# Post-norm decoder layer on one core: cross attention, routing and shared expert written as one stage

## The reference, cut to what matters

```python
x = _layernorm(x + _L0_attn_ref(x, Wq, bq, Wk, bk, Wv, bv, Wo, bo))      # 16 heads of 128, 4 KV heads
x = _layernorm(x + _L0_xattn_ref(x, ctx, ctx, Wh, wg_w, wo_w, gn_gamma, gn_beta))
x = _layernorm(x + _L0_ffn_ref(x, gate_weight, inv_mapping, ...))

def _L0_xattn_ref(x, k, v, Wh, wg_w, wo_w, gn_gamma, gn_beta):             # 2 heads of 128
    Q, K, V = (einsum('bshd,hde->bshe', t, Wh) for t in (xh, kh, vh))
    scores = einsum('bshe,bthe->bhst', Q, K) / sqrt(hd)
    A = maximum(abs((scores * Dn).sum(axis=0)), 1.0)        # summed over all 16 sequences
    O = einsum('hst,bthe->bshe', A, V)
    Y = (O - mu) / sqrt(var + GN_EPS) * gn_gamma + gn_beta
    return relu(x @ wg_w) * Y @ wo_w

def _moe_forward(x, ...):                                   # 64 routes, top 6, 8 experts of 8
    scores = softmax(x @ gate_weight.T)
    w_dense = the 6 largest of 64, the others 0
    flat = w_dense[:, inv_mapping]                          # (tokens, 8 experts, 8)
    scalar = flat.sum(-1)
    soft = softmax(where(flat == 0, -1e9, flat), axis=-1)   # the second softmax
    y = sum over f of scalar[f] * expert_f(x, soft[f])
    return y + silu(x @ sh_gate_W.T) * (x @ sh_up_W.T) @ sh_down_W.T      # + the shared expert
```

## Time and profile before

| what | us |
|---|---|
| three timed runs | 960.9, 962.25, 964.76; median 962.25 |
| the profiled execution | 962.09, of which the traced span is 960.2 |
| TensorE busy | 893.3 (93%) |
| VectorE, ScalarE, GpSimd busy | 654.8, 518.3, 370.9 |
| identity products of `keep_busy` in the cross stage (L57) | 120 instructions, 14.2 |

### The profile page before, as it was taken

One profiled execution on the slowest core, in us unless ns is written; L12 is line 12 of the kernel. 1 busy time (PEld: TensorE's weight loads), 2 busy tenths in 40 slices (PEclk: granted clock), 3 DMA queues, 4 the chain that ended last, 5 costly groups with the idle time before them and its releaser, 6 DMA issues. The chain is left out here.

```text
span 960.2 us, 16062 instructions
## 1 busy us (share of the span) xinstructions
PE 893.3 (93%) x5722; PEld 797.7 (83%) x5722; DVE 654.8 (68%) x1347; ACT 518.3 (54%) x1225; POOL 370.9 (39%) x261
## 2 busy tenths in 40 slices
PE   6899999999999999899789888999999999999992
PEld 5799999999999998777678786888888888888882
DVE  4656564656565565657758865778887888787885
ACT  4655555647464555214444326566656566666553
POOL 1721212213131312025424225474747465657430
PEclk9999999999999999999999999999999999999996
DMA  6300000000000000400010020202202020200002
GB/s 222 110 2 23 1 22 0 22 0 22 7 15 11 0 12 1 135 1 1 1 65 6 8 98 31 85 29 79 79 29 86 31 87 22 85 23 23 23 1 88
DMA packets 16430, 38.00 MB, mean 40 GB/s; under 512 B 2048, under 2 KB 6912, under 8 KB 15232
## 3 DMA queue, kind: packets, MB, share of 16 engines
q1 hardware_dynamic: 15744, 35.29, 10.8%
q0 software_dynamic: 640, 2.10, 0.7%
HBM read 34.76 MB, written 2.62 MB: 39 GB/s over the span
## 5 line engine op out<-in xcount | busy, mean ns | idle before, releaser
L241 POOL TENSOR_TENSOR att_probs<-att_probs,att_share 128x512 f32<-128x512 f32 x64 | 66.3, 1039 | 191.6 <-DVE att_share L525 191.6
L1491 POOL TENSOR_TENSOR all_xT_lo<-moe_inner,all_xT_lo 128x512 fp32r<-128x512 f32 x64 | 82.7, 1292 | 89.5 <-ACT all_xT_lo L1668 86.2
L429 ACT ACTIVATE att_probs<-att_score,att_bias 128x128 f32<-128x128 f32 x256 | 90.5, 380 | 41.9 <-DVE att_bias L516 41.7
L1483 POOL TENSOR_TENSOR all_xT_hi<-moe_xe,all_xT_hi 128x1024 fp32r<-128x1024 f32 x31 | 74.5, 2403 | 65.4 <-ACT all_xT_hi L1627 65.4
L1668 ACT ACTIVATE all_xT_lo<-moe_inner 128x512 fp32r<-128x512 f32 x64 | 40.4, 631 | 89.2 <-DVE moe_inner L1738 89.2
L562 DVE SCALAR_TENSOR_TENSOR att_OT_lo<-att_mix,att_bv,att_OT_hi 128x512 fp32r<-128x512 f32 x64 | 45.8, 750 | 58.1 <-ACT att_OT_hi L467 58.1
L467 ACT ACTIVATE att_OT_hi<-att_mix,att_bv 128x512 fp32r<-128x512 f32 x64 | 43.5, 703 | 65.9 <-PE att_mix L50 65.7
L48 PE MATMUL att_proj<-att_xT_hi,att_Wq_hi 128*128 128x256 f32 x256 | 74.8, 292 | 1.4 <-DVE att_Wq_lo L490 0.8
L48 PE MATMUL att_acc<-att_Wo_hi,att_OT_hi 128*128 128x256 f32 x256 | 73.0, 285 | 1.6 <-DVE att_OT_lo L562 1.6
L302 PEld LDWEIGHTS att_score<-att_KT,att_QT 128*128 128x128 f32 x512 | 62.5, 196 | 11.8 <-issue 8.6
L50 PE MATMUL att_proj<-att_xT_hi,att_Wq_lo 128*128 128x256 f32 x256 | 72.1, 281 | 0.0
(11 more groups left out here) (299 smaller groups left out, 2904.7 us busy)
## 6 DMA issues: line engine op xcount, KB each, us to landing
all_stage<-in_expert_w SPq DMA_DIRECT2D x8, 1152.0 KB, 5.1
moe_spread<-soft_dram SPq DMA_DIRECT2D x64, 128.0 KB
all_scale<-in_expert_scale SPq DMA_DIRECT2D x8, 320.0 KB, 5.4
att_xT<-in_xT SPq DMA_DIRECT2D x8, 256.0 KB, 3.1
att_stage<-in_Wq SPq DMA_DIRECT2D x4, 512.0 KB, 7.4
att_stage<-in_Wo SPq DMA_DIRECT2D x4, 512.0 KB, 5.4
att_x_tok<-in_x_tok POOLq DMA_DIRECT2D x8, 256.0 KB, 3.1
out<-all_r SPq DMA_DIRECT2D x4, 512.0 KB, 4.4
```

What stands on the lines that cost most here:

```text
L241: pool.tensor_tensor(p3, p3, each, ALU.mult).then_inc(prob_ready, 1)
L429: ins = act.activation(p_[:, c], score[b][:, c], ACT.Exp, bias=bias[b][:, h:h + 1], scale=SCALE, accum_out=m_[:, h:h + 1])
L1483: pool.tensor_tensor(xe[u % 2].lo[:, :], xe32[:, :], xe[u % 2].hi[:, :].bitcast(F32), ALU.subtract).then_inc(xe_lo, 1)
L1491: pool.tensor_tensor(innerT[u % 2].lo[at], inner[at], innerT[u % 2].hi[at].bitcast(F32), ALU.subtract).then_inc(inner_lo, 1)
```

## The change

The cross and route functions become one, `cross_and_route`, with one order per engine and no barrier between them.

- SyncE issues in this one stage: the context, `decay`, `gamma` and `beta` (now 2 values per partition each), `route_w` without the router's columns, the router's columns `Wr`, then `inv` and `rows`. VectorE's program for the stage begins with the wait for the last two, their two instructions and four memsets. Among them are `ln_eps` and `gn_eps`, which ScalarE waits for (`eps_ready`) before its first square root.
- The gates come out transposed (features on partitions). The normalised mix is turned instead of the gated product, and gamma and beta are applied by ScalarE on the way out of PSUM, with a scale and a bias per partition; before, GpSimd did that with two passes over broadcast copies.
- The square roots take the epsilon as a bias, so VectorE's additions of it go.
- The group norm's factors come in groups of 2, 2, 4, 4 and 4 tiles, and the last layer norm in groups of 2.
- All of `keep_busy` in the merged stage goes; those of the attention's end and of the experts' start stay.
- The second softmax is written once; ScalarE copies the turned result three times (high part twice, and the fp32 copy for DRAM) where it copied once, and VectorE drops a copy.
- The shared expert's next slices are put between the steps of routing, and `kept` is copied out by ScalarE.
- The first expert's weights are split in eight parts on GpSimd, one behind each low half.
- In the first turn of the attention the projections of Q2 stand before the second set of scores.
- In the experts `move_low` stands behind the unit's first SiLU.

```diff
@@ -336,6 +336,10 @@
 
                 for j in range(KV):
 
+                    if j == 0 and weights:
+                        pe.wait_ge(w_lo, j + 5)
+                        for what in step_units(j, last):
+                            projects(what)
                     if not (last and j == KV - 1):
 
                         for q_unit in ((-3, -2), (1, 2), (3, 4), (7, 8))[j]:
@@ -356,11 +360,9 @@
                             mm = pe.transpose(mix[b][:, h * S:(h + 1) * S], probs[j % 2][b][:, h * S:(h + 1) * S],
                                               ident[:, :])
                         mm.then_inc(pt_ready, 1)
-                    if j == 0 and weights:
-                        pe.wait_ge(w_lo, j + 5)
                     if j == 2 and not last:
                         pe.wait_ge(xT_lo, g + 2)
-                    if j != 1:
+                    if j > 1 or j == 0 and not weights:
                         for what in step_units(j, last):
                             projects(what)
...
         @block.sync
         def _(sp):
             for c in range(1, CHUNKS):
-                sp.dma_start(ctxT[c][:, :].rearrange("p (h t) -> p h t", h=XH),
+                sp.dma_start(ctxT[c].rearrange("p (h t) -> p h t", h=XH),
                              a["ctxT"][:, :, c * CT:(c + 1) * CT]).then_inc(ctx_in[c], 16)
-            sp.dma_start(decay[:, :], a["decay"]).then_inc(const_in, 16)
+            sp.dma_start(decay, a["decay"]).then_inc(const_in, 16)
             for dst, src in ((gamma, a["gamma"]), (beta, a["beta"])):
-                sp.dma_start(dst[:, :], src.rearrange("(o d) -> o d", o=1).to_broadcast([P, D])).then_inc(const_in, 16)
-            sp.dma_start(w32[:, :], a["route_w"]).then_inc(route_in, 16)
+                sp.dma_start(dst[:, :], src.rearrange("(k p) -> p k", k=DK), allow_slow_non_contiguous=True
+                             ).then_inc(const_in, 16)
+            sp.dma_start(w32[:, :], a["route_w"][:, DK * E:]).then_inc(route_in, 16)
+            sp.dma_start(Wr[:, :], a["route_w"][:, 0:DK * E]).then_inc(wr_in, 16)
+            sp.dma_start(inv_raw[:, :], a["inv"].rearrange("(o e) -> o e", o=1).to_broadcast([E, FK])).then_inc(small_in, 16)
+            sp.dma_start(rows[:, :], a["rows"]).then_inc(small_in, 16)
+            sp.wait_ge(route_lo, 1)
+            load_weights(sp, a, 0, stage, scale, expert_in)
+            by_parity = soft_dram.rearrange("(f two k) t -> two f k t", two=GROUPS, k=F)
+            for c in range(CHUNKS):
+                for n in range(GROUPS):
+                    sp.wait_ge(softT32_ready, GROUPS * c + n + 1)
+                    sp.dma_start(by_parity[n, :, :, c * CT:(c + 1) * CT], softT32[:, n * CT:(n + 1) * CT]).then_inc(stored, 16)
+                if c == CHUNKS - 2:
+                    sp.wait_ge(expert_ready, 1)
+                    load_weights(sp, a, 1, stage, scale, expert_in)
+            sp.wait_ge(stored, 16 * GROUPS * CHUNKS)
+            sp.wait_ge(expert_in, 64)
 
         @block.gpsimd
...
-            keep_busy(pe, bank[7], ident, 14)
 
...
-            gates(0, (0,))
-            pe.wait_ge(at_ready, 1)
-            mix_values(0)
-            gates(0, (1,))
-            mix_values(1)
-            keep_busy(pe, bank[4], ident, 8)
-            mix_values(2)
-            keep_busy(pe, bank[4], ident, 14)
...
+            pe.wait_ge(at_ready, 1)
+            mix_values(0)
+            mix_values(1)
+            gates(0)
+            for c in range(CHUNKS):
+                turn_mix(c)
+                if c < CHUNKS - 2:
+                    mix_values(c + 2)
+                if c:
+                    turn_x2(c - 1)
+                outputs(c)
+                if c < CHUNKS - 1:
+                    gates(c + 1)
...
+            shared_in(0, 0)
+            shared_in(0, 1)
+            logits(0)
             for i in range(2):
                 pe.wait_ge(turned2_lo, 2 * (CHUNKS - 2) + i + 1)
-            keep_busy(pe, bank[0], ident, 14)
             turn_x2(CHUNKS - 1)
-            keep_busy(pe, bank[0], ident, 10)
+            shared_in(0, 2)
+            for c in range(CHUNKS):
+                if c < CHUNKS - 1:
+                    shared_in(c + 1, 0)
+                turn_kept(c)
+                if c < CHUNKS - 1:
+                    shared_in(c + 1, 1)
+                flat(c)
+                if c == CHUNKS - 2:
+                    logits(c + 1)
+                shared_out(c)
+                if c < CHUNKS - 2:
+                    logits(c + 1)
+                if c < CHUNKS - 1:
+                    shared_in(c + 1, 2)
+                soft_out(c)
...
-            act.activation(gram[:, :], bank[4][:, 0:HH], ACT.Copy).then_inc(gram_out, 1)
-            act.wait_ge(var_ready, 1)
-            act.activation(std[:, :], var[:, :], ACT.Sqrt).then_inc(std_ready, 1)
+            act.activation(gram, bank[4][:, 0:HH], ACT.Copy).then_inc(gram_out, 1)
+            act.wait_ge(eps_ready, 2)
+            act.wait_ge(mv_ready, 1)
+            act.activation(std[:, :], mv2[:, :, 1], ACT.Sqrt, bias=ln_eps[:, 0:1]).then_inc(std_ready, 1)
             for n in range(0, 4 * CHUNKS, 2):
                 act.wait_ge(kv_ready, n + 1)
                 act.activation(kv_to(n), bank[n % 4][:, :], ACT.Copy).then_inc(kg_out, 1)
...
+            def affine(c):
+
+                if c == 0:
+                    act.wait_ge(const_in, 48)
+                for i in range(2):
+                    act.wait_ge(y_turned, 2 * c + i + 1)
+                    if c:
+                        act.wait_ge(wyt_out, 2 * (c - 1) + i + 1)
+                    for k in range(DK):
+                        at = slice(k * 2 * P, (k + 1) * 2 * P)
+                        ins = act.activation(YT[i][:, at], bank[4 + i][:, at], ACT.Identity, bias=beta[:, k:k + 1],
+                                             scale=gamma[:, k:k + 1])
+                    ins.then_inc(yt_out, 1)
...
+            def soft_high(c):
+                for n in range(GROUPS):
+                    act.wait_ge(soft_turned, GROUPS * c + n + 1)
+                    for at in (0, 2 * GR):
+                        ins = act.activation(softT[n][at:at + GR, c * CT:(c + 1) * CT], soft_bank[n][0:GR, :], ACT.Copy)
+                    if c:
+                        act.wait_ge(stored, 16 * GROUPS * c)
+                    act.activation(softT32[:, n * CT:(n + 1) * CT], soft_bank[n][0:GR, :], ACT.Copy
+                                   ).then_inc(softT32_ready, 1)
+
+            for n in (CHUNKS - 1, CHUNKS):
+                deviation(n)
+                normalise_x2(n)
+            shared(0, 0)
+            shared(0, 1)
+            exp1(0)
+            for i in range(2):
+                high_x2(2 * (CHUNKS - 1) + i)
+            shared(0, 2)
+            for c in range(CHUNKS):
+                if c < CHUNKS - 1:
+                    shared(c + 1, 0)
+                take_kept(c)
+                if c < CHUNKS - 1:
+                    shared(c + 1, 1)
+                exp2(c)
+                if c < CHUNKS - 1:
+                    exp1(c + 1)
+                    shared(c + 1, 2)
+                soft_high(c)
...
-                dve.wait_ge(mv_ready, n)
-                at = slice(tiles[0], tiles[-1] + 1)
-                dve.tensor_scalar(var[:, at], mv2[:, at, 1], LN_EPS, None, ALU.add).then_inc(var_ready, 1)
-
-            variance(range(B), 1)
+
+            dve.wait_ge(small_in, 32)
+            dve.tensor_copy(inv[:, :], inv_raw[:, :]).then_inc(inv_ready, 1)
+            dve.wait_ge(inv_ready, 1)
+            dve.tensor_scalar(onehot[:, :], inv[:, :], rows[:, 0:1], None, ALU.is_equal).then_inc(onehot_ready, 1)
+            dve.memset(s3[:, :, E:E + 1], 3.0).then_inc(sentinels, 1)
+            dve.memset(s3[:, :, E + 1:E + 2], 2.0).then_inc(sentinels, 1)
+            dve.memset(ln_eps[:, :], LN_EPS).then_inc(eps_ready, 1)
+            dve.memset(gn_eps[:, :], GN_EPS).then_inc(eps_ready, 1)
+            moments(range(B), 0)
             dve.wait_ge(std_ready, 1)
             dve.reciprocal(rstd[:, :], std[:, :]).then_inc(rstd_ready, 1)
             dve.wait_ge(rstd_ready, 1)
...
-                for copy in range(3):
-                    to = soft2[:, :].rearrange("p (t n c) -> p n t c", t=TT * GROUPS, n=3)[:, copy]
-                    ins = dve.tensor_tensor(to.rearrange("p t (f k) -> p t f k", k=F), four(e2[:, :]),
-                                            four(part2[:, :]).to_broadcast([P, TT * GROUPS, F // GROUPS, F]), ALU.mult)
-                ins.then_inc(soft2_ready, 1)
-            shared_out(CHUNKS - 2)
-            for n in range(GROUPS):
-                split_soft(CHUNKS - 1, n)
-            shared_out(CHUNKS - 1)
+                dve.tensor_tensor(soft2[:, :].rearrange("p (t k) -> p t k", k=F), e2_8, wide(part2, TT * F, F), ALU.mult
+                                  ).then_inc(soft2_ready, 1)
+
+            factors_x2(CHUNKS - 1)
+            variance(CHUNKS)
+            factors_x2(CHUNKS)
```

(27 more changed lines are left out.)

913 lines of the change are left out of this document (448 added, 465 removed).

## The result

The changed kernel takes 985.45 us (median of 4 runs, 984.1 to 986.77), the kernel before 961.88 in the same job. The ratio is 1.0229 (95% interval 1.0203 to 1.0255), so it is 2.3% slower. The prediction was 976.6 us with a range of 962 to 985. The direction and the main cause were right; the size was 8.9 us short. The time is 0.45 us past the upper end of the range; the ratio, laid on the 962.25 us from which the forecast started, gives 984.3 us, just inside.

What follows compares the result with a forecast made beforehand. No engine is full in the stages that merge; chains passing from engine to engine bound them. 962.09 + 0.6 + 12.9 - 6.5 + 1.8 + 2.0 + 3.7 = 976.6 us, range 962 to 985, likeliest case 970 to 982.

Steps and rivals of the forecast that it cites:

- The start of the stage: Merged stage's head: VectorE waits for late `inv` and `rows`, then for GpSimd's hold on the shared port; +12.9 us.
- else +1.3: Merged stage's head: extra if ScalarE's table load of 1.28 us before the root came in line, not beside.
- The bound of +15: Upper bound for the stage's start: every small load waits as `decay` did and the table load is in line.
- From `AT` to the last output: From `at_ready` to the last output product: fillers and GpSimd's passes gone, 49.0 us against 55.65; -6.5 us.
- From there to the experts: Last output product to the experts: barrier and fillers gone, longer chunk periods, earlier first chunk; +1.8 us.
- the three periods: Routing chunks, `flat` to `flat`: 19.5 us each against 18.0, since ScalarE and VectorE get more work; +4.5 us.
- Port and clock: Routing chunks: VectorE meets GpSimd on the port oftener and TensorE's clock falls without filler; +2.0 us.
- The third rival: Routing chunks: three more clock drops of 1.7 us and 3 us more of port, 984.7 us; chance 0.15.
- The experts: Experts stage: `move_low` behind the SiLU lengthens TensorE's wait for moved rows in seven units; +3.7 us.
- The attention's +0.6: Attention: Q2's projections ahead of the second scores make those scores late, partly given back later; +0.6 us.
- the merged stage bound by matmuls: Rival, behind `at_ready`: TensorE's work alone sets the time, 122 to 123 us against 145.35, total 957; chance 0.11.
- The kept routing period: Rival, routing chunks: the period falls to 16.9 us and nothing meets on the port, total 966.2; chance 0.13.

Runs made afterwards that it cites:

- early_loads: Changed kernel with SyncE issuing `inv` and `rows` ahead of the context; 973.61 us, ratio 1.0108.
- pool_late: Changed kernel with GpSimd's split of the shared expert's weights waiting until VectorE's comparison and memsets are done, loads still late; 982.17 us, ratio 1.019.
- fill: Changed kernel with identity products put back at four waits of the merged stage; 978.49 us, ratio 1.0177.
- best: Changed kernel with late_pool's edits, swap_back, att_back, fillers as in fill (last chunk's moved), and the second softmax ahead of shared slice k = 2; 951.33 us, ratio 0.9871.
- before_nofill: Kernel before with the six `keep_busy` calls of its cross and route stages left out; 970.22 us, ratio 1.0048.
- swap_back: Changed kernel with the move of 48 rows ahead of a unit's first SiLU again; 981.25 us, ratio 1.0199.
- best_tail: best with 40 identity products added behind TensorE's last instruction of the merged stage, ahead of the barrier; 951.33 us, ratio 0.9864.
- att_back: Changed kernel with the attention's earlier order, Q2's projections behind the first turn's second scores; 984.79 us, ratio 1.0225.
- late_pool: Changed kernel with VectorE's `inv` and `rows` instructions behind its last turned-x copy, and GpSimd's weight split behind the last normalisation; 964.3 us, ratio 1.0011.
- before_pool: Kernel before with GpSimd's split of the shared expert's weights waiting for VectorE's last normalisation; 962.39 us, ratio 0.9995.

## Why the prediction was right, and where its sizes were off

**The start of the stage** was right as a mechanism and in place, in both halves: the late loads (early_loads) and the port (pool_late) are each shown by an edit that changes nothing else. That all loads of one queue pass in the order of their issue was not right: `inv` landed ahead of `route_w`; it made no difference, since `rows` came last. The forecast, which counted from 391.69, had GpSimd's end 20.1 us behind the stage's start; it was 19.0. The stretch was 1.9 us longer than forecast all the same: the table load of 1.28 came in line and not beside, though that was written down as "else +1.3", and the path from piece 4 to the second sum of scores took 15.6 us (415.88 to 431.48) for the 13.5 forecast. Of these 2.1 the twelve pieces hold 0.9 (12.9 us for 12.0: they started at half clock for longer than was reckoned), and the turn of x and the first sum of scores 1.2 (2.7 for 1.5). The bound of +15 held it.

**From `AT` to the last output** was forecast as -6.5 and measured -2.3. The chain itself was well read: in fill, where the clock stays up, the stretch is 46.15 + 3.46 = 49.6 us against the forecast's 49.0. What is missing is the clock: two drops, 1.8 and 1.7 us.

**From there to the experts** was +5.7 for +1.8, and here is the term of the sum that was furthest off. The first `flat` was to come 2.7 us earlier behind the last output; it comes 2.0 later (22.5 us for 20.5). The gain was there at first: the logits start 5.5 us behind the last output and not 8.1. But from the logits to `flat` it takes 17.0 us for 12.4. In the trace 1.7 of these 4.7 us are the product of 2.15 us beside GpSimd; the low half of x stands ahead of the sum of the exponentials on VectorE, and ScalarE has more ahead of the copy of `kept`. TensorE waits 3.7 us there. The first `flat` stands as late in fill and best (both 22.5), and no run of mine undid it, so how these parts add up is left open. Against that the three periods cost 2.1 us where 4.5 were forecast (18.7 each for 19.5). Behind the last `flat` it is 17.0 us for 15.5: that is clock, since it is 15.0 in fill.

**Port and clock** was sized wrongly too: +2.0 was "one more drop and 0.3 of port", and by fill the clock alone cost 5.7, in three places, beside the 1.7 of port in the first chunk. The third rival (three more drops, port 3) came nearest in time, with 984.7 us, though two of the drops lie ahead of the routing chunks where it put them all. The row at 503.41 in the earlier trace rows had the price of a drop, 1.7; what I got wrong was how often. I argued that slices of the shared expert would fill TensorE's idle times, but in the chunks ahead of routing and behind the last `flat` there are no such slices, and fillers or full clock stood there before. before_nofill shows the same in the other kernel: leaving the fillers out costs 0.5%.

**The experts** were +5.0 for +3.7: the swap is +3.3 to 3.4, by the waits and by swap_back. The rest is 1.5 us. The half clock at the stage's start does not explain it by itself: in early_loads and pool_late the first product takes the same 0.76 us, and their experts take 393.0 us, 3.0 more than before and not 5.0; in best they take 390.2. best_tail mends the start and shortens nothing. So for those 1.5 us I have no shown cause.

**The attention's +0.6** wasn't seen: att_back has the same time, and executions differ by over 1 us there.

Of the other rivals, the merged stage bound by matmuls (957 us) was far off: TensorE is busy in 75.2 of 95.6 us behind the last output. The kept routing period (966) was off by 1.8 us a chunk (18.7 for 16.9), and by all that lies around it.

The total owes something to luck and to a wide range. Its likeliest stretch, 970 to 982, did not hold the result. Terms that were too small by 14.8 us in sum (attention 1.1, start 1.9, up to the last output 4.2, first `flat` 4.7, behind the last `flat` 1.5, experts 1.3) met 4.4 us that were too much (the periods 2.4, and 2.0 for port and clock, whose real cost is in the other lines).

## What to carry to other kernels

Where stages are merged, look first at what the head of each in-order engine waits for: two small instructions, and the waits in front of them, on data that nobody wants for another 100 us cost 14.6 us because the whole stage stood behind them. If GpSimd must do a long pass, put it where VectorE copies out of PSUM (late_pool); delaying it by less than 3 us (pool_late) handed the lock to VectorE's next instruction. And when fillers go, look at every wait that they stood in: left bare, waits of 2.4 to 4.7 us were followed by work at half clock, and a port lock of which 2.0 us could be won before then cost 5.8 us.

## What the runs showed that I had not expected

A lock is handed on: pool_late took 4.8 us from one instruction and 4.1 came back at another. A filler and a stall at the same place cost only the longer of the two, so that taking either away alone wins little (2.0 us for the same edit in before_pool, 5.8 in late_pool). And a full clock at a stage's start can be worth nothing: in best_tail 1.2 us were won in the first 10 us of the experts, and 0.2 were left at the end of the stage.
